# Graph network on one core: when VectorE adds the first layer to the gathered rows

## The reference

```python
x   = concat(h[src], h[dst], edge_weight)      # 2*256 + 1 per edge
msg = silu(x @ mW1 + mb1)                      # first layer
msg = layer_norm(msg, ln_g, ln_b)
msg = silu(msg @ mW2 + mb2)                    # second layer
agg = segment_sum(msg, src, num_segments=3125)
```

## Time and profile before

| | |
|---|---|
| median of 3 runs | 2164.03 us (2155.17 to 2167.69) |
| profiled execution | 2147.24 us, its span 2145.5 us |
| busy over the span: PE, PEld, DVE, ACT, POOL | 1842.9, 1596.6, 1813.8, 1584.3, 1400.0 us |
| first and last add (L1219) start | 371.4 and 1828.0 us |
| mean granted clock of TensorE | 0.953 of 2.4 GHz |

### The profile page before, as it was taken

One profiled execution on the slowest core, in us unless ns is written; L12 is line 12 of the kernel. 1 busy time (PEld: TensorE's weight loads), 2 busy tenths in 40 slices (PEclk: granted clock), 3 DMA queues, 4 the chain that ended last, 5 costly groups with the idle time before them and its releaser, 6 DMA issues. The chain is left out here.

```text
span 2145.5 us, 48204 instructions
## 1 busy us (share of the span) xinstructions
PE 1842.9 (86%) x11549; PEld 1596.6 (74%) x11550; DVE 1813.8 (85%) x4667; ACT 1584.3 (74%) x3326; POOL 1400.0 (65%) x1293
## 2 busy tenths in 40 slices
PE   3556752599999999999999999999999999999996
PEld 2335542588888888888888888888888888777784
DVE  5999985588898998898889888898888989655995
ACT  2547763488898998898889888898888989723321
POOL 5566766777777777887777777787777887003000
PEclk9978985699999999999999999999999999999998
DMA  4000102443333333333333333333333336101001
GB/s 131 1 3 30 34 27 95 122 157 95 95 99 97 97 97 95 100 99 97 100 96 95 98 97 96 97 98 94 99 96 93 100 95 93 45 1 24 7 1 60
DMA packets 109682, 169.22 MB, mean 79 GB/s; under 512 B 42642, under 2 KB 79428, under 8 KB 109374
## 3 DMA queue, kind: packets, MB, share of 16 engines
q0 software_dynamic: 43168, 114.55, 20.3%
q1 hardware_dynamic: 61504, 48.91, 7.4%
q10 hardware_dynamic: 4954, 5.08, 0.7%
HBM read 156.30 MB, written 11.74 MB: 78 GB/s over the span
## 5 line engine op out<-in xcount | busy, mean ns | idle before, releaser
L1005 POOL DMA_INDIRECT g_rows<-b_table,idx_ring x816 | 905.9, 1110 | 293.3 <-issue 237.1
L1126 PE MATMUL ps<-w2g,nT 128*128 128x256 f32 x3432 | 825.0, 384 | 39.3 <-ACT rec L1027 31.9
L1126 PEld LDWEIGHTS ps<-w2g,nT 128*128 128x128 f32 x3432 | 622.4, 191 | 125.3 <-issue 54.3
L1034 ACT ACTIVATE normed<-act,rec 128x255 f32<-128x255 f32 x858 | 468.8, 602 | 42.7 <-PE psM L1118 16.6
L1219 DVE TENSOR_TENSOR g_rows<-psH,g_rows 128x512 f32<-128x512 f32 x429 | 293.2, 683 | 118.8 <-remote 58.8
L1098 PE MATMUL psH<-a_sb,ohT 128*128 x1716 | 348.5, 326 | 33.2 <-issue 18.5
L1225 DVE BATCH_NORM_STATS2 rec<-act 128x6 f32<-128x256 f32 x858 | 319.3, 413 | 57.4 <-ACT act L1048 44.7
L1098 PEld LDWEIGHTS psH<-a_sb,ohT 128*128 128x128 f32 x1716 | 260.7, 194 | 85.7 <-issue 66.5
L1044 ACT ACTIVATE nT<-psM 128x512 f32<-128x512 f32 x429 | 254.3, 593 | 77.9 <-PE ps L1126 39.1
L1027 ACT ACTIVATE rec<-ps 128x512 f32<-128x512 f32 x429 | 256.9, 599 | 55.7 <-PE psG L1109 36.7
L1231 DVE TENSOR_TENSOR low<-rec,high 128x512 fp32r<-128x512 f32 x429 | 289.2, 674 | 7.1 <-ACT high L1040 7.1
(11 more groups left out here) (203 smaller groups left out, 2326.4 us busy)
## 6 DMA issues: line engine op xcount, KB each, us to landing
loc_rows<-loc_d SPq DMA_DIRECT2D x143, 187.5 KB
g_rows<-b_table,idx_ring POOLq DMA_INDIRECT x816
h_sb<-in_x SPq DMA_DIRECT2D x1, 3125.0 KB
b_table<-b_out SPq DMA_DIRECT2D x25, 125.0 KB
x_all<-in_x ACTq DMA_DIRECT2D x1, 3125.0 KB
out<-x_all SPq DMA_DIRECT2D x5, 625.0 KB
ohT<-ew_d SPq DMA_DIRECT2D x143, 9.0 KB
idx_ring<-rec SPq DMA_DIRECT2D x136, 3.0 KB
```

Source lines behind the costliest of these rows:

```text
L1005: pool.indirect_dma_start(g_rows[:, j, n, :], None, b_table[:, :], bass.IndirectOffsetOnAxis(ap=which, axis=0)).then_inc(s_gather[j], 16)
L1034: ins = nc.scalar.activation(normed[:, (j - 10) % 2, n, 0:D - 1], act1[:, (j - 10) % RING, n, 0:D - 1], ACT.Identity, scale=rstd_e[:, g % ...
L1126: mm = pe.matmul(ps2[:, (j - 13) % 2, n, :], nT[:, (j - 13) % 2, n, q, :], w2g[:, q, :], start=(q == 0), stop=(q == 1))
```

## The change

The add in slot t works on pair t-3 instead of t-2. It reads the half of `psH` that belongs to that pair, and waits for the first layer and the gathers of that pair. All else stays, the lag of `act1` and of the statistics too.

```diff
                     shifts(t, d, j)
-                    if has(t, 2):
-                        k = (j - 2) % RING
-                        dve.wait_ge(s_first, t - 1)
-                        dve.wait_ge(s_gather[k], 32 * (d + 1 if j >= 2 else d))
-                        V.tensor_tensor(g_rows[:, k, :, :], psH[:, j % 2, :, :], g_rows[:, k, :, :],
+                    if has(t, 3):
+                        k = (j - 3) % RING
+                        dve.wait_ge(s_first, t - 2)
+                        dve.wait_ge(s_gather[k], 32 * (d + 1 if j >= 3 else d))
+                        V.tensor_tensor(g_rows[:, k, :, :], psH[:, (j - 3) % 2, :, :], g_rows[:, k, :, :],
                                         ALU.add).then_inc(s_hid, 1)
```

## The result

The changed kernel takes 2247.8 us (median of 4 runs, 2246.28 to 2251.66). The kernel before, on the same chip, takes 2165.86 us (4 runs). The ratio is 1.039, with a 95% interval from 1.0363 to 1.0417: slower by 3.9%, some 82 us. The profiled execution took 2246.49 us, its span 2244.8, at a granted clock of 0.955.

The account below looks back on a forecast made before the run. TensorE was taken as the bound, 95% busy, with VectorE and ScalarE close behind. 65 us lost less 3 won gave +62, of which two thirds, +41, should stay: 2205 us, own range 2176 to 2235, 8-in-10 range 2150 to 2255.

Parts of the forecast that it names:

- Step (a): VectorE's add needs the first layer one slot earlier: most of its 113 us wait goes, worth 3 us to TensorE.
- Step (b): Gathered rows get one more slot to land before the add: between -5.5 us and 0, taken as 0.
- Step (c): ScalarE's act1 L1048 waits for the add of one slot before instead of two; 3.2 us of cover, taken as 0.
- Step (d): TensorE's next first layer must wait for the current slot's add, 1.01 us later, 64 times: 65 us lost.
- Every group of three slots pays: Rival: VectorE never gets ahead, so all 143 groups delay TensorE's first layer by 1.01 us: +144 us, 2308 us; chance 0.06.
- The part absorbed: TensorE's waits for ScalarE before L1126 and L1118 (66 us) swallow a third of the 62 us, leaving +41.
- ScalarE's waits: Sign in the profile after: ScalarE's waits before L1027 and L1044 should not shrink by more than a third.
- The doubt on the size that the forecast named: If late marks keep their own time, not TensorE's, its waits for ScalarE give back what the later first layer takes.
- Weight loads before L1098: Sign: TensorE's weight-load idle time before the first layer rises from 58.1 to about 110 us in the steady stretch.

Follow-up runs that it names:

- the gate alone: Kernel before, add unmoved, but TensorE's first layer of slot t waits for the add of slot t-1 instead of t-2: 2232.01 us against 2151.0, ratio 1.0388.
- the long pause: Kernel before, with a 256-column memset that GpSimd waits for behind the third gather of each six: 2169.65 us against 2165.01, ratio 1.0025.

## Why the prediction was right in kind and half in size

The forecast was 2205 us, 41 over 2164; it became 2247.8, 82 over 2165.86. Slower was right. The wide range, up to 2255, held it; the forecast's own, up to 2235, did not. The wide range had been stretched for slots without a wait, so it held for another reason than the one given.

- **Step (a), right.** VectorE's idle time before L1219 fell over the whole kernel from 118.8 us to 23.2 (forecast: under 30), and TensorE gained nothing by it: the gate alone costs as much as the gate with the relief. The running sum, where the forecast also looked for waits, has hardly any (7.7 us in the middle).
- **Step (b), right.** The waits for gathered rows went from 5.5 to 4.8 us.
- **Step (c), right.** 1.0004 alone.
- **Step (d), right in place and near in price, wrong in number. This is the step that failed.** TensorE waits before L1098, and the add ends that wait (123 times, 100.1 us, 0.81 us each). The forecast had 64 waits of the statistics at 1.01 us. After the change there are 133 of them:

```profile
  ACT act L1048: 208.4, 133
```

  133 x 1.01 = 134 us. I had counted the waits of the kernel before and held the count fixed. But the count itself depends on the change. My reading is a circle: a second layer whose mark comes late holds ScalarE's transposed copy, act1 is then late for VectorE, VectorE's add is late for TensorE, and TensorE's next second layer is late again. Before, the gate was a slot away and this circle was open; now it closes in nearly each of the 143 groups of three slots. The timeline above shows one turn of it, and the two kernels that shorten or open it, the add moved up and the third `nT`, give time back; that it is the whole of the doubling is argued and not shown. There are no more late marks than before (502 of 1322 on record over 1 us late, 544 of 1431 before). More of them fall where an engine stands waiting. "Every group of three slots pays" was the rival given 0.06; its count came true, though not its cause. It was to come from a VectorE that never gets ahead by itself, 0.18 us after the next first layer; the experiments show that late marks are needed for it (the two orders are level where no mark is late).
- **The part absorbed.** The forecast let a third of the sum pass into TensorE's waits for ScalarE. Over the whole kernel the idle time of TensorE before L1126 and L1118 fell from 39.3 + 27.4 to 17.7 + 7.9 us, by 41. 134 - 41 = 93 us, against 99 us measured in the spans. So the two terms that carry the result are 134 where I had 65 - 3, and -41 where I had -21. That sum mixes a price from one round with measured idle time, and its closeness is in part luck. The rows of the weight loads over the whole kernel add up without a price:

```profile
L1098 PEld LDWEIGHTS psH<-a_sb,ohT 128*128 128x128 f32 x1716 | 260.7, 194 | 85.7 <-issue 66.5
...
L1098 PEld LDWEIGHTS psH<-a_sb,ohT 128*128 128x128 f32 x1716 | 245.3, 193 | 241.7 <-issue 235.4
```

  The first is before, the second after: +156.0 us at the gate. Before L1126 and L1118 their idle time fell from 125.3 + 33.3 to 106.4 + 9.2 us, by 43.0, and the busy time of all weight loads by 14.1 (1596.6 to 1582.5). 156.0 - 43.0 - 14.1 = 98.9 us. By these rows the term of step (d) is 156 us where the forecast had 65.
- **ScalarE's waits** should not shrink by more than a third. The one before L1044 grew from 77.0 to 206.1 us in the middle, but the one before L1027 shrank by two thirds, so this sign held for one and failed for the other:

```profile
L1027 ACT ACTIVATE rec<-ps 128x512 f32<-128x512 f32 x408 | 244.2, 598 | 52.7 <-PE psG L1109 33.8 <-remote 16.0 <-issue 3.0
...
L1027 ACT ACTIVATE rec<-ps 128x512 f32<-128x512 f32 x382 | 227.5, 596 | 15.8 <-remote 10.8 <-PE psG L1109 2.5 <-issue 2.5
```

  The first is before, the second after. The wait moved from one instruction of ScalarE to another, and in sum it grew. The doubt on the size that the forecast named, late marks that keep their own time, would have made the loss smaller; it became larger.
- **Weight loads before L1098**: 110 us forecast, 200.0 measured; slot 3.50 forecast, 3.63 measured. Both are step (d)'s count again.

The rule to take the fullest engine and end its gaps, of the Trainium skill's page "Perfetto Trace Analysis" (sections "Identifying the Most-Contended Engine" and "Optimization Strategy"), would have given 2051 us. Most of VectorE's gap at the add did go, 96 of 119 us, and the kernel became 3.9% slower: the measurement decides against the rule here. VectorE's gap was not work that was missing but the far end of TensorE's slack.

Why the marks are late I had left open. Shown: they are on time when the indirect gathers are replaced by plain transfers, from either issuer, at the same traffic, and when there is one gather a pair, most of them with idle time before it. The delays get shorter, and don't vanish, when GpSimd's run of six gathers is broken by a long enough pause. Open: what in a close run of gathers holds them, and whether the scattered rows have a part in it. Of the marks, it is TensorE's that are late; those of VectorE, ScalarE and GpSimd stand on record 0.01 us after the end of nearly every instruction, with the gathers too. The Trainium skill's page "Perfetto Trace Analysis" (section "Tensor Engine Instruction") says that the profile estimates the end of a matmul and that TensorE raises its mark only once PSUM has acknowledged the writes. The traces with plain transfers agree that the estimate is near, with every mark on record within 0.02 us of it. A mark raised on PSUM's acknowledgement would explain why a held one shows as a gap and not as a longer matmul; no run here looks at PSUM itself.

## What to carry to other kernels

Before an edge is moved in a loop of several engines, walk the circle: if A waits for B, B for C and C for A, and the edge takes the last slack out of it, the number of waits in the profile before is no count for the profile after; price it for each turn of the loop too, and give that case real weight. A large idle time in front of an instruction may be slack that an engine elsewhere lives on. And where a mark comes late for no reason that the instructions show, look at what GpSimd does meanwhile, and try the kernel once with that replaced, before tuning the order around it. A wait that vanishes is no proof that its mark is on time: another wait may have taken its place, as under the long pause.

## What the hardware showed that I had not expected

- Indirect gathers on GpSimd that follow one another 0.30 us apart go with marks of TensorE that come late and then several at once: about a quarter of those on record by more than 2 us (342 of 1431 before the change, 364 of 1322 after). With half the gathers, most of them after some 1.5 us of idle time, none was. In this kernel the difference is 7%: 2008.19 us with plain transfers of the same bytes, 2165.01 with gathers, though TensorE, VectorE and ScalarE do the same work.
- GpSimd issues a plain transfer in 548 ns and an indirect gather in 1110 to 1131 ns, 128 rows each.
- No version with the real gathers went clearly past the kernel before. The best is the kernel before with three `nT` buffers, 0.8% faster (0.9923 [0.9896, 0.9951]).
